# A transformer layer on one core: rounded query and key parts moved ahead of their remainders, and the first group's turn, keys and head norms put in another order

## The reference, cut to what matters

```python
x = x + attn(layernorm(x)); x = x + ffn(layernorm(x))
# inside attn, for each token:
q, k, v = split(ternary_linear(x, w_qkv))          # 256 + 64 + 64 columns
q, k = rms_norm(q), rms_norm(k)                    # over the 16 features of a head
q, k = apply_rotary_emb(q, cos, sin), apply_rotary_emb(k, cos, sin)
q = q * q_gain
scores = einsum('bqhgd,bkhd->bhgqk', q, k) / 4     # causal
y = einsum('bhgqk,bkhd->bqhgd', softmax(scores), v)
```

## Time and profile before

| | us |
|---|---|
| median of 3 runs | 587.46 |
| lowest and highest of them | 583.75 and 588.2 |
| the profiled execution's own time | 586.47 |
| its span, first to last instruction | 584.7 |
| outside the span | 1.77 |

### The profile page before, as it was taken

The page is one execution under the profiler, slowest core; times in us unless marked ns, Lnnn a source line. Parts: engine busy times, 40 slices in busy tenths (PEclk is TensorE's granted clock), DMA queues, the critical chain, the costliest instruction groups (busy, mean ns, idle before and its releaser), DMA issues.

```text
span 584.7 us, 9812 instructions
## 1 busy us (share of the span) xinstructions
PE 474.4 (81%) x3202; PEld 265.1 (45%) x3202; DVE 314.9 (54%) x886; ACT 362.2 (62%) x567; POOL 171.1 (29%) x222
## 2 busy tenths in 40 slices
PE   1693949898999999999398978848888789999930
PEld 1581313333333333333143523326767679888930
DVE  6963615843732148031266485445948657666626
ACT  4244839897999999999359566615252335555520
POOL 3711100002110111103242145045455814444430
PEclk9878869999999999999789888868988989999975
DMA  7111011974799649624421113211111424444349
GB/s 207 36 42 41 2 40 30 278 204 107 214 298 296 164 77 4 2 53 110 138 57 62 26 46 114 62 34 64 30 55 40 123 73 119 117 119 128 101 132 353
DMA packets 77526, 61.37 MB, mean 105 GB/s; under 512 B 26984, under 2 KB 70600, under 8 KB 77480
## 3 DMA queue, kind: packets, MB, share of 16 engines
q1 hardware_dynamic: 73784, 51.04, 37.5%
q0 software_dynamic: 3408, 9.34, 4.4%
q10 hardware_dynamic: 288, 0.39, 0.3%
HBM read 19.88 MB, written 29.34 MB: 84 GB/s over the span
## 4 chain that ended last, share of the span: by engine, by line
PE 44%; DVE 15%; issue 13%; SPq 8%; DMA 7%; ACT 6%; POOL 5%; another core or an unknown queue 1%; ACTq 0%; POOLq 0%; DVEq 0%
PE ps L1548 14%; PE ps L1528 10%; PE ps L1720 6%; ACT prob L772 5%; SPq L445 4%; PE ps L1738 3%; POOL rows_by_expert L649 2%; PE ps L1468 2%; SPq L366 2%; PE ps L1557 1%; DMA qk<-qT 1%; PE ps L1711 1%; DMA yfin<-pair_out 1%; PE ps L1742 1%; PE ps L1489 1%
## 5 line engine op out<-in xcount | busy, mean ns | idle before, releaser
L772 ACT ACTIVATE prob<-ps 128x1024 f32<-128x1024 f32 (+3 forms) x320 | 260.1, 922 | 76.1 <-PE ps L1528 69.1
L1548 PE MATMUL ps<-prob,v_sb 128*32 128x512 f32 (+3 forms) x1280 | 156.8, 564 | 17.8 <-DVE o_sb L1048 9.0
L1528 PE MATMUL ps<-qk 64*128 64x512 f32 (+3 forms) x640 | 122.5, 448 | 24.1 <-DMA qk<-qT 15.3
L608 POOL TENSOR_SCALAR_AFFINE_SELECT prob<-prob 128x512 f32<-128x512 f32 x64 | 41.6, 652 | 233.7 <-ACT prob L772 232.8
L1528 PEld LDWEIGHTS ps<-qk 64*128 64x128 f32 x640 | 54.5, 194 | 118.2 <-ACT prob L772 82.2
L1548 PEld LDWEIGHTS ps<-prob,v_sb 128*32 128x32 f32 x1280 | 25.9, 110 | 65.1 <-issue 34.7
L710 POOL DMA_INDIRECT pair_out<-yo,xg x39 | 37.5, 963 | 56.1 <-DVE yo L1404 55.8
L1048 DVE COPY o_sb<-ps 128x512 f32<-128x512 f32 x16 | 11.0, 690 | 67.7 <-PE ps L1548 67.2
L1666 PE MATMUL ps<-x2T,ws_hi 128*128 128x512 f32 (+1 forms) x96 | 33.0, 428 | 5.4 <-DVE hid L1273 5.4
L649 POOL DMA_INDIRECT rows_by_expert<-xs,slots x32 | 31.2, 976 | 14.2 <-issue 8.6
L1036 DVE CAST qT<-ps 96x512 fp32r<-96x512 f32 x16 | 11.0, 686 | 38.6 <-PE ps L1489 38.6
(11 more groups left out here) (203 smaller groups left out, 781.2 us busy)
## 6 DMA issues: line engine op xcount, KB each, us to landing
rows_by_expert<-pads SPq DMA_DIRECT2D x9, 1935.0 KB, 20.4
qk<-qT SPq DMA_DIRECT2D x138, 64.0 KB, 2.1
xg<-rows_by_expert SPq DMA_DIRECT2D x39, 129.0 KB
yfin<-pair_out SPq DMA_DIRECT2D x8, 512.0 KB, 7.1
stage<-in_w SPq DMA_DIRECT2D x8, 352.0 KB
x_sb<-in_x SPq DMA_DIRECT2D x4, 512.0 KB, 6.8
qk<-shT SPq DMA_DIRECT2D x8, 256.0 KB, 4.8
res<-in_x SPq DMA_DIRECT2D x4, 512.0 KB, 4.1
```

Source lines behind the costliest of these rows:

```text
L608: nc.gpsimd.affine_select(out=t, in_=t, compare_op=ALU.is_ge, fill=0.0, base=0, pattern=[[0, HPG], [1, P]], channel_multiplier=-1).then_in ...
L772: nc.scalar.activation(prob[:, u % NPB, 2 * hf:2 * hf + 2, c0:CH], ps[:, b:b + 2, c0:CH], ACT.Exp, scale=SCALE).then_inc(exp_done, 1)
L1528: ins = M(ps[:, 2 * (n % NSB) + h, c0:CH], qk[rows, par, PAIRS, kt * P:(kt + 1) * P], qk[rows, par, hf, j * CH + c0:(j + 1) * CH], start=T ...
L1548: ins = M(ps[VW * h:VW * (h + 1), O_BANK, c0:CH], v_sb[:, kt, :], prob[:, u % NPB, h, c0:CH], start=(kt == 0), stop=(u == LAST_OF[j]), ski ...
```

## The change

Five edits, none of which changes what is computed:

- The moves of a chunk are issued in two parts. VectorE raises a new semaphore `hi_taken` right after hi; SP then issues the DMAs that read hi (four for the queries, two for the keys), waits for `x_free`, and issues those that read lo (two and one). `K_PARTS` and `Q_PARTS` keep their values under new names. `first_keys` on ScalarE's queue is split in the same way. This holds for all chunks of all groups.
- Chunk 1 of the first group is turned after step 0, not after step 1 (`FIRST_GROUP`).
- Its keys are issued behind the exponentials of block 3, not ahead of them.
- `norm_qk` is split into `squares_qk` (squares and sum) and `scale_qk` (the rest). For chunk 1 the squares go ahead of `low_part_x(3)`, and so does the rounding of the projection weights; for chunks 2 and 3 the squares go ahead of `take_round(0, 1)`.
- `moved` is written in another form with the same value.

```diff
-    1: [("round", 0, 1)], 4: [("out", 0, 0)], 8: [("round", 0, 2)], 12: [("out", 0, 1)], 16: [("round", 0, 3)],
+    0: [("round", 0, 1)], 4: [("out", 0, 0)], 8: [("round", 0, 2)], 12: [("out", 0, 1)], 16: [("round", 0, 3)],
...
-                sp.wait_ge(x_free, round_use(g, c))
-                cs = slice(c * CH, (c + 1) * CH)
-                for hf in range(2):
-                    for n, part in enumerate(Q_PARTS):
-                        sp.dma_start(qk_f[n:P:4, (g + 1) % 2, hf, cs],
-                                     qT_f[2 * HD * hf:2 * HD * (hf + 1), part, cs]).then_inc(ld_qk[c], 16)
-                if g > 0 or c >= K_BY_ACT:
-                    move_k(sp, g, c, ld_qk[c])
+                for want, ready, at in ((HI, hi_taken, NC * g + c + 1), (LO, x_free, round_use(g, c))):
+                    sp.wait_ge(ready, at)
+                    for hf in range(2):
+                        move_q(sp, g, c, hf, want, ld_qk[c])
+                    if g > 0 or c >= K_BY_ACT:
+                        move_k(sp, g, c, want, ld_qk[c])
...
             def first_keys(c):
+                act.wait_ge(hi_taken, c + 1)
+                move_k(nc.scalar, 0, c, HI, ld_first_k[c])
                 act.wait_ge(x_free, round_use(0, c))
-                move_k(nc.scalar, 0, c, ld_first_k[c])
+                move_k(nc.scalar, 0, c, LO, ld_first_k[c])
...
-                if u == TPC - 1:
+                if u == TPC:
                     first_keys(1)
                 exps(0, u)
...
                 link(V.tensor_copy(hi, ps[0:QKD, X_BANK, :]))
+                dve.sem_inc(hi_taken, 1)
                 V.tensor_tensor(lo, ps[0:QKD, X_BANK, :], hi.bitcast(F32), ALU.subtract).then_inc(x_free, 1)
...
             low_part_x(2)
-            low_part_x(3)
             round_weights(1, D // P)
             dve.wait_ge(qkv_ready, 2 * TPC)
-            norm_qk(0, TPC, 2 * TPC)
+            squares_qk(0, TPC, 2 * TPC)
+            low_part_x(3)
+            scale_qk(0, TPC, 2 * TPC)
             dve.wait_ge(qkv_ready, NT)
             values(0)
             rotate(TPC, 2 * TPC)
+            squares_qk(0, 2 * TPC, NT)
             for c in range(1, NC):
                 take_round(0, c)
                 if c == 1:
                     copy_output(0, 0)
-                    norm_qk(0, 2 * TPC, NT)
+                    scale_qk(0, 2 * TPC, NT)
                     take_output(0, 0)
```

More of the change, by code:

```diff
@@ L56 @@
 QKD = (HS + 1) * HD
-Q_PARTS, K_PARTS = (0, 1, 0), (0, 0, 1)
+HI, LO = 0, 1
+Q_PARTS, K_PARTS = (HI, LO, HI), (HI, HI, LO)
 MOVES = 2 * len(Q_PARTS) + len(K_PARTS)
@@ L114, in moved @@
 def moved(g, c):
-    return 16 * ((MOVES + (2 if c == 0 else 0)) * (g + 1)) - 16 * (len(K_PARTS) if c < K_BY_ACT else 0)
+    return 16 * (MOVES + (2 if c == 0 else 0)) * (g + 1) - (16 * len(K_PARTS) if c < K_BY_ACT else 0)
 ORDER = [v for u in sorted(LAST_GROUP) for v in LAST_GROUP[u]] + [v for u in sorted(AFTER) for v in AFTER[u]]
@@ L304, in build @@
         ones_ready = sem("ones_ready")
+        hi_taken = sem("hi_taken")
         ld_qk = [sem(f"ld_qk{c}") for c in range(NC)]
@@ L360, in build, with move_q, move_k @@
         qk_f, qT_f, shT_f = (t[:].bitcast(F32) for t in (qk, qT, shT))
-        def move_k(queue, g, c, done):
+        def move_q(queue, g, c, hf, want, done):
+            cs = slice(c * CH, (c + 1) * CH)
+            for n, part in enumerate(Q_PARTS):
+                if part == want:
+                    queue.dma_start(qk_f[n:P:4, (g + 1) % 2, hf, cs],
+                                    qT_f[2 * HD * hf:2 * HD * (hf + 1), part, cs]).then_inc(done, 16)
+        def move_k(queue, g, c, want, done):
             cs = slice(c * CH, (c + 1) * CH)
             for n, part in enumerate(K_PARTS):
-                queue.dma_start(qk_f[n:P:4, (g + 1) % 2, PAIRS, cs], qT_f[HPG * HD:QKD, part, cs]).then_inc(done, 16)
+                if part == want:
+                    queue.dma_start(qk_f[n:P:4, (g + 1) % 2, PAIRS, cs], qT_f[HPG * HD:QKD, part, cs]).then_inc(done, 16)
         def step_use(n, j):
@@ L987, in _, with columns_qk, squares_qk, scale_qk @@
             half = HD // 2
-            def norm_qk(g, t0, t1):
+            def columns_qk(g, t0, t1):
+                q = qkv[:, t0:t1, bass.ds(g * HPG * HD, HPG * HD)].rearrange("p t (h d) -> p t h d", d=HD)
+                return q, qkv[:, t0:t1, bass.ds(g * HD + NH * HD, HD)]
+            def squares_qk(g, t0, t1):
                 nt = t1 - t0
-                q = qkv[:, t0:t1, bass.ds(g * HPG * HD, HPG * HD)].rearrange("p t (h d) -> p t h d", d=HD)
-                k = qkv[:, t0:t1, bass.ds(g * HD + NH * HD, HD)]
-                a, b = wk_a[:, t0:t1], wk_b[:, t0:t1]
+                q, k = columns_qk(g, t0, t1)
+                a = wk_a[:, t0:t1]
                 V.tensor_tensor(a[:, :, 0:HPG, :], q, q, ALU.mult)
                 link(V.tensor_tensor(a[:, :, HPG, :], k, k, ALU.mult))
-                n = nt * HS
-                link(V.tensor_reduce(sm[:, 4, 0:n], a.rearrange("p t h d -> p (t h) d"), AX, ALU.add))
+                link(V.tensor_reduce(sm[:, 4, 0:nt * HS], a.rearrange("p t h d -> p (t h) d"), AX, ALU.add))
+            def scale_qk(g, t0, t1):
+                nt, n = t1 - t0, (t1 - t0) * HS
+                q, k = columns_qk(g, t0, t1)
+                b = wk_b[:, t0:t1]
                 rs = rsqrt(n, sm[:, 4, 0:n], 1.0 / HD, RMS_EPS).rearrange("p (t h) -> p t h", h=HS)
@@ L1004, in norm_qk @@
                 link(V.tensor_tensor(b[:, :, HPG, :], k, rs[:, :, HPG:HS].broadcast_to([P, nt, HD]), ALU.mult))
+            def norm_qk(g, t0, t1):
+                squares_qk(g, t0, t1)
+                scale_qk(g, t0, t1)
             def rotate(t0, t1):
```

## The result

| | before | changed kernel |
|---|---|---|
| median of 22 runs each, same chip | 588.26 us | 584.15 us |
| lowest to highest | 583.75 to 592.43 | 578.95 to 587.99 |
| the profiled execution's own time | 586.47 | 584.15 |

The ratio is 0.9921 with a 95% interval of 0.9898 to 0.9944: 4.6 us of 588.26 (3.3 to 6.0). That lies within 1% and beside the forecast's 581.2 / 586.47 = 0.9910. The median of 584.15 is inside the range.

What follows compares the result with a forecast made beforehand. TensorE's work fills attention, so its waits for query and key DMAs (15.3 us) and a VectorE copy (9.0) bound it. Terms 2.24 + 1.22 + 0.48 + 0.65 + 0.65 = 5.24 us off 586.47 give 581.2; range 578.3 to 585.4.

Steps and rivals of the forecast that it cites:

- Hi first: In every chunk SP starts issuing at hi's end instead of lo's, so the whole row moves 0.65 us earlier.
- rival A: Lo's DMAs land no sooner, so issuing hi ahead buys nothing at five places; 584.3 us, chance 0.11.
- The turn one step sooner: First group, chunk 1: the turn takes the place of block 3's scores, 49.47 instead of 50.81, gaining 1.34 us.
- rival E: If VectorE had not rotated chunk 1 in time, block 3's scores wait behind the turn; no chance of its own.
- 0.25 in the projection: Chunk 0's keys issued from hi free ScalarE's copies sooner, so TensorE's 0.25 us wait at 36.62 goes.
- Squares ahead: First group, chunk 2: VectorE's rotation no longer holds the turn, which starts near 71.34, 0.57 us sooner.
- rival C: The clock helps: shorter gaps mean one or two fewer blocks at 1.2 GHz, about 579.2 us; chance 0.15.
- The mask beside the squares: Chunk 1's squares may delay GpSimd's first mask: at most 0.22 us by the rows, 0.68 by the skill; taken 0.
- Chunk 3: First group: 0.65 off the 1.08 us wait, less 0.17 returned waiting for VectorE's copy; 0.48 us booked.
- The last group: SP's unbroken queue starts at hi, bringing weight pieces, rounding and the copy forward: 0.65 us off the 9.03 wait.
- Rival B: Small waits at chunk 3, the second and last groups are replaced by the next late thing; 583.0 us, chance 0.17.
- rival D: The clock hurts: the shifted program meets more 1.2 GHz stretches, about 2 us each, ending slower than before; chance 0.07.

Runs made afterwards that it cites:

- the repeat: The changed kernel itself once more, nothing edited: 581.52 us against 588.47 for the kernel before, ratio 0.988.
- hi first alone: The kernel before with only hi issued ahead of lo in every chunk; turn, keys and norms in the old order: 584.53 us against 587.68, ratio 0.9957.
- The run with the norms in one piece: The changed kernel with chunk 1's squares and the rounding of projection weights back behind `low_part_x(3)`: 589.96 us, one execution.
- the order alone: The changed kernel with both parts issued after lo and `hi_taken` not raised, other edits kept: 585.4 us against 587.68 for the kernel before, ratio 0.9978.

## Why the prediction was right, and where its steps were off

- **Hi first.** Right, and by the measured means the larger half, though the two intervals overlap. Alone it gives 2.5 us (0.9 to 4.1) where its terms make 5 x 0.65 - 0.17 = 3.08. The 0.09 that I deducted lies on SP's side: from hi to SP it takes 0.08 (51.04 to 51.12), from lo it took 0.01 (52.92 to 52.93). Raising `hi_taken` moves lo back by another 0.12: lo starts 0.15 behind hi's end (51.19), before 0.03, and nothing waits for it. The landing stays at 2.07, so rival A is out for the chunks of the first group and the second group's first. What the forecast did not have is the idle time of VectorE in the second group, which takes 0.36 back there and 0.12 in the third.
- **The turn one step sooner.** Right at 2.4 GHz, by one pair of profiles: 1.92 of 1.99 between the first scores and chunk 1's, which hold this and hi first. The rotation was through in time, so rival E did not come up. Its size hangs on the clock: 2.0 us instead of 1.34 where the clock has already fallen.
- **0.25 in the projection.** That ScalarE's copies come sooner is right: the first one behind the three issues starts 4.04 us after chunk 0's turn (31.92 to 35.96), before 4.70 (31.39 to 36.09). What TensorE makes of it hangs on the clock and is not shown. The wait at 36.62 did go in this profile, and from the turn to the first scores it takes 12.79 instead of 13.19; but 0.29 of these 0.40 can be one step of the projection fewer at 1.2 GHz (0.64 against 0.35). In the repeat a wait of 0.17 is left, in hi first alone, where TensorE is at 2.4 GHz there, one of 1.22, and the stretch varies from 12.54 to 13.78 in the eleven experiments with hi first, against 13.21 in the one without. The profile's start, up to chunk 0's turn, was 0.53 later, which differs from profile to profile; hence the -0.13 in the ledger.
- **Squares ahead.** The mechanism was right: the wait for the rotation is gone. The term was 0.57, and the pair of single runs gives 0.74, where the clock is back early; where it comes back late the place is worth nothing. The other 0.3 of the 1.68 in this stretch is the clock, which rose at about 60.3 us and not at 63.6. This is rival C in the forecast's smallest form. It did not come once more anywhere, as C had wanted.
- **The mask beside the squares.** I took 0 where the Trainium skill's rule would have given up to 0.68. In the changed kernel they miss each other by 0.08 us, so 0 is right here. In all other profiles but one the first mask has its 0.64 as well. The run with the norms in one piece is that one and shows what a meeting costs: 0.44 on the mask, twice the 0.22 that I had as the upper bound from 19 masks. It is less than the whole square, since the square was under way when the mask came. The bound was too low, and the choice held by a narrow margin, which is luck as much as working.
- **Chunk 3.** The give-back was forecast at 0.17; the product starts 4.01 us behind chunk 3's scores (100.41 to 104.42), 3.86 before, and right at the copy's end (104.37): 0.15. It falls into the stretch behind chunk 3, and chunk 3 and the second group make 1.29 together against 1.13.
- **The last group.** The wait went from 9.03 to 8.32, and the stretch from the turn to the product shrank by 0.70, against 0.65. But neither carries the term: over all profiles of kernels that leave this place alone the wait lies between 7.42 and 9.05, while the rounding starts 3.8 to 5.1 us behind the issue of the weight pieces, and the order alone, without hi first, had 8.42 and a stretch of 38.50. What is shown is the start of the queue: from the turn to the round's first issue 2.29 us before and 1.63 after. How much of this lead is left when the queue reaches the weight pieces differs: it takes 30.82 us from the turn before, 30.74 with the order alone, 30.29 after, and 30.07 to 30.76 in the other runs with hi first. So the lead is 0.5 in the profile of the change and 0.1 or less in three others, which is what rival A had said of this queue: there it sets its own pace for a while. The 0.65 of this term stays open.
- **Rival B.** It is out for chunk 3 and the second group's first scores: their waits fell by 0.66 and 0.81, and these two stretches keep 1.29. In small it did come, at a place that it did not name: the second group's copy, above.
- **Behind 291 us.** The profile of the change keeps 4.98 us up to there and 2.5 at the end. TensorE's stretches at 1.2 GHz in the last group lie elsewhere, and a wait for `x2T` is 2.8 instead of 0.6; this is what rival D had as its place. From the last group's product to the end of the span it takes 293.35 us before and 295.83 after, but 292.74 in the repeat and 291.61 to 298.76 in the other experiments on these chips, so one profile's end proves little. The 22 executions keep 4.6 of about 5 us, so on the mean little is given back. How much of the 2.5 us is the change's doing and how much is this one execution stays open. The wait for `x2T` is 2.1 to 2.9 in the eight experiments on chips where the kernel before takes 587.68 to 588.47, whichever half of the change they hold, and is absent from the list in the four on the chip where it takes 580.95; of the kernel before there is one profile only.

So the forecast of 5.24 lay 0.6 above the 4.6 measured, inside its interval (3.3 to 6.0). Up to the last group's product the single pair of profiles gives 4.98 against 5.24. That these two are so near is in part luck: 0.3 of the clock came to the gain at chunk 2, 0.48 went in the second and third group, and neither was in the sum.

## What to carry to other kernels

Where a wait ends with the last of a row of DMAs that one queue issues 0.64 us apart, start the queue on the first data that is ready and order the issues so that the rest is needed late; the whole row moves by that much and no landing changes. Judge a step moved at a clock boundary by the start of the next fixed event behind it and not by the wait ahead of it: here the wait shrank by 0.9 us in a stretch that took 1.5 us longer. And before you take a wait away, look at what the same engine has to deliver next: of three waits that shrank by 9.9 us together, 4.4 us reached the end.

## What the runs showed of the hardware that was not expected

- TensorE's clock is not the same in each run of a program. In 9 of the 12 other profiles it had fallen to 1.2 GHz by 46 to 49 us, between the projection and chunk 1's turn, where the rows of before and of the change stay at 2.4 GHz. In the repeat it costs 1.5 us up to chunk 1's scores (13.16 against 11.64). In this thin stretch TensorE pauses for 1.05 and 0.48 us only before it falls.
- A mask on GpSimd and a square on VectorE that overlap lengthen each other by 0.44 us each (1.08 against 0.64, 0.72 against 0.28).
- Chips differ by more than the change is worth: the kernel before has a median of 580.95 us on one and 587.68 to 588.47 on the others, so only ratios on the same chip count. In the two profiles from the faster chip whose last group is as in the change, the difference lies behind the last group's product: 286.08 and 287.02 us from there to the end against 291.61 to 298.76 elsewhere, with the product itself at 285.5 against 284.8 to 291.4.
- Raising a semaphore by an instruction of its own between two VectorE instructions puts 0.12 us between them: 0.15 from hi's end to lo's start instead of 0.03. With hi first taken out it is 0.03 again.
